# A graph network's second layer: attention scores scaled four tiles at a time and scattered from the features' block

## What is computed

```python
Qh = (x @ Wq + bq).reshape(N, 8, 32)
Kh = (x @ Wk + bk).reshape(N, 8, 32)
Vh = (x @ Wv + bv).reshape(N, 8, 32)
s = einsum('nhc,nhc->nh', Qh, Kh) / sqrt(32)      # one score for a node and head
alpha = leaky_relu(s[src] + s[dst], 0.2)          # edges, and one loop for each node
e = exp(alpha - segment_max(alpha, dst)[dst])
a = e / segment_sum(e, dst)[dst]
attn = segment_sum(Vh[src] * a[:, :, None], dst)
```

## Time and profile before

| | us |
|---|---|
| median of 3 runs | 2505.18 |
| lowest and highest | 2496.7, 2505.32 |
| the profiled execution's own time | 2504.01 |
| its span (first to last instruction) | 2502.2 |
| busy: PE, DVE, Pool, ACT | 1745.7, 1753.9, 1411.1, 597.9 |
| mean granted TensorE clock, as a share of full speed | 0.859 |

### The profile page before, as it was taken

One profiled execution on the slowest core, in us unless ns is written; L12 is line 12 of the kernel. 1 busy time (PEld: TensorE's weight loads), 2 busy tenths in 40 slices (PEclk: granted clock), 3 DMA queues, 4 the chain that ended last, 5 costly groups with the idle time before them and its releaser, 6 DMA issues. The chain is left out here.

```text
span 2502.2 us, 36831 instructions
## 1 busy us (share of the span) xinstructions
PE 1745.7 (70%) x10655; PEld 1385.5 (55%) x10655; DVE 1753.9 (70%) x2694; ACT 597.9 (24%) x1285; POOL 1411.1 (56%) x1456
## 2 busy tenths in 40 slices
PE   2698016788665654999987999020588899758498
PEld 1576014566444443899886777020456666547487
DVE  6688714899655557555686888970479999877675
ACT  2465100000000003455423333040011111124464
POOL 4377877777777772000006777887777777720050
PEclk9799556999978787899988999565789999979799
DMA  4166454666433342000022667536466666430100
GB/s 152 46 192 223 161 175 124 209 211 205 120 106 106 106 105 69 1 1 0 18 80 74 206 203 248 167 102 218 121 211 212 207 212 209 142 99 1 40 12 34
DMA packets 118702, 320.74 MB, mean 128 GB/s; under 512 B 37112, under 2 KB 63120, under 8 KB 104810
## 3 DMA queue, kind: packets, MB, share of 16 engines
q0 software_dynamic: 62272, 170.01, 23.8%
q1 hardware_dynamic: 55754, 145.31, 16.4%
q10 hardware_dynamic: 608, 4.59, 0.5%
HBM read 248.70 MB, written 71.12 MB: 128 GB/s over the span
## 5 line engine op out<-in xcount | busy, mean ns | idle before, releaser
L1214 PE MATMUL ms_ps_m<-ms_msg,ms_pick 128*128 128x260 f32 (+1 forms) x2816 | 794.5, 434 | 392.1 <-DVE ms_msg L1197 189.3
L804 POOL DMA_INDIRECT e_ring<-table,e_index x840 | 795.4, 947 | 257.8 <-issue 254.7
L1214 PEld LDWEIGHTS ms_ps_m<-ms_msg,ms_pick 128*128 128x128 f32 x2816 | 572.4, 212 | 613.9 <-issue 511.8
L1197 DVE TENSOR_TENSOR ms_msg<-e_ring,ms_ps_w 128x1040 f32 (+1 forms) x352 | 438.8, 1247 | 338.4 <-SPq L1138 338.4
L843 POOL DMA_INDIRECT e_ring<-table,e_stage_index x416 | 474.2, 1140 | 125.9 <-issue 120.6
L694 PE MATMUL sc_ps_e<-sc_keys,sc_hot 125*128 125x100 bf16 (+1 forms) x3840 | 290.2, 229 | 7.4 <-DVE all_xn L642 4.3
L694 PEld LDWEIGHTS sc_ps_e<-sc_keys,sc_hot 125*128 125x128 bf16 x3840 | 254.7, 98 | 54.0 <-DVE all_xn L642 25.1
L1180 DVE SCALAR_TENSOR_TENSOR ms_pick<-graph_dst_col,graph_tile_base,ms_ps_lane 128x512 f32<-128x512 f32 x352 | 263.2, 748 | 0.8 <-DVE all_acc L1167 0.8
L642 DVE TENSOR_REDUCE all_xn<-sc_ps_e 128x800 f32 (+1 forms) x240 | 236.0, 985 | 17.9 <-PE sc_ps_e L694 12.0
L605 ACT ACTIVATE sc_rows<-sc_ps_b 125x512 bf16<-125x512 f32 x320 | 173.0, 596 | 248.6 <-PE sc_ps_b L682 223.9
L1189 DVE TENSOR_TENSOR all_acc<-all_acc,ms_ps_m 128x260 f32 (+1 forms) x352 | 152.0, 432 | 55.2 <-PE ms_ps_m L1214 55.0
(11 more groups left out here) (423 smaller groups left out, 2652.1 us busy)
## 6 DMA issues: line engine op xcount, KB each, us to landing
ahead<-e_ring SPq DMA_DIRECT2D x32, 1056.0 KB, 4.6
e_ring<-ahead SPq DMA_DIRECT2D x32, 1056.0 KB, 5.1
ahead<-e_ring SPq DMA_DIRECT2D x20, 1040.0 KB
e_ring<-ahead SPq DMA_DIRECT2D x20, 1040.0 KB, 5.2
e_ring<-table,e_index POOLq DMA_INDIRECT x840, 2.8
e_ring<-table,e_stage_index POOLq DMA_INDIRECT x416
w_w<-L_ffn_w SPq DMA_DIRECT2D x2, 2048.0 KB
table<-qkv_v SPq DMA_DIRECT2D x5, 528.0 KB, 3.0
```

What stands on the lines that cost most here:

```text
L804: pool.indirect_dma_start(out=g.ring[:, slot * QUAD + i // GT, i % GT, :], out_offset=None, in_=s.table[:, :], in_offset=bass.IndirectOffs ...
L1197: dve.tensor_tensor(msg[:, b, :, 0:R].rearrange("p t (h o) -> p t h o", h=H), ring[:, bass.ds(slot, 1), :, :].rearrange("p a t (h o) -> p ...
L1214: mm = pe.matmul(ps_m[q % BANKS][:, 0:W], pick[:, b, t, :], msg[:, b, t, :], start=t == 0, stop=t == GT - 1)
```

## The change

The scatter of one tile's scores becomes a function, `place_score`. For layer one nothing moves: `edge_scores` calls it 20 times at the head of Pool's list as before. For layer two (`placed` is true there) `edge_scores` leaves it out, and Pool has a list of its own in the features' block: for each group of four tiles it waits for `score_ready` and issues four scatters. DVE scales four tiles at a time, after the fourth one's sum, in place of all 20 at the end, and each scaling counts `score_ready` up by one; the splitting and SP's store of the scores wait for all five. The numbers that are computed are the same.

```diff
--- before.py
+++ after.py
@@ -555,7 +555,13 @@
                 sp.wait_ge(h_out, 16 * (NT // step + 1))
 
 
-def edge_scores(nc, s, block, between, stage, tag, edge, parts, node, node_dram, line, dst_line, dst_start, H):
+def place_score(pool, line, first_edge, node, a, scattered):
+
+    pool.indirect_dma_start(out=line[:, :], out_offset=bass.IndirectOffsetOnAxis(ap=first_edge[:, a:a + 1], axis=0),
+                            in_=node[:, a, :], in_offset=None).then_inc(scattered, 16)
+
+
+def edge_scores(nc, s, block, between, stage, tag, edge, parts, node, node_dram, line, dst_line, dst_start, H, placed):
 
     C = HI * H
     SLOT = P if C <= P else 2 * P
@@ -581,9 +587,9 @@
 
         @block.gpsimd
         def _(pool):
-            for a in range(NT):
-                pool.indirect_dma_start(out=line[:, :], out_offset=bass.IndirectOffsetOnAxis(ap=s.first_edge[:, a:a + 1], axis=0),
-                                        in_=node[:, a, :], in_offset=None).then_inc(scattered, 16)
+            if not placed:
+                for a in range(NT):
+                    place_score(pool, line, s.first_edge, node, a, scattered)
             pool.indirect_dma_start(out=dst_start[:, :], out_offset=None, in_=node_dram[:, :],
                                     in_offset=bass.IndirectOffsetOnAxis(ap=s.chunk_dst[:, :], axis=0)).then_inc(scattered, 16)
 
@@ -1548,10 +1554,19 @@
                     dve.tensor_tensor(q_row[:, b, :], q_row[:, b, :], k_row[:, b, :], ALU.mult).then_inc(qk_ready, 1)
                     dve.wait_ge(qk_ready, a + 1)
                     dve.tensor_reduce(score[:, a, :], q_row[:, b, :].rearrange("p (h o) -> p h o", o=O), AX.X, ALU.add).then_inc(dot_ready, 1)
-                dve.wait_ge(dot_ready, NT)
-                link(dve.tensor_scalar(score[:, :, :], score[:, :, :], float(O) ** -0.5, None, ALU.mult))
-                dve.sem_inc(score_ready, 1)
+                    if a % SUB == SUB - 1:
+                        dve.wait_ge(dot_ready, a + 1)
+                        tiles = slice(a - SUB + 1, a + 1)
+                        dve.tensor_scalar(score[:, tiles, :], score[:, tiles, :], float(O) ** -0.5, None, ALU.mult).then_inc(score_ready, 1)
+                dve.wait_ge(score_ready, NB)
                 split_scores(dve, link, score, parts, rest)
+
+            @block.gpsimd
+            def _(pool):
+                for a in range(NT):
+                    if a % SUB == 0:
+                        pool.wait_ge(score_ready, a // SUB + 1)
+                    place_score(pool, s.lines[1], s.first_edge, score, a, s.scattered["sc1"])
 
             @block.sync
             def _(sp):
@@ -1562,7 +1577,7 @@
                 for a in range(0, NT, step):
                     sp.wait_ge(v_ready, a + step)
                     sp.dma_start(node_view(s.table[a * P:(a + step) * P, :]), v[:, a:a + step, :, :].rearrange("p a h o -> p a (h o)")).then_inc(v_out, 16)
-                sp.wait_ge(score_ready, 1)
+                sp.wait_ge(score_ready, NB)
                 sp.dma_start(node_view(s.dst_scores[1]), score[:, :, :]).then_inc(v_out, 16)
                 sp.wait_ge(v_out, 16 * (NT // step + 2))
 
@@ -2324,7 +2339,7 @@
 
         with nc.Block() as block:
             picks = edge_scores(nc, s, block, between, stage, "sc" + layer, edge, parts, node, s.dst_scores[int(layer)], s.lines[int(layer)],
-                                dst_line, dst_start, H)
+                                dst_line, dst_start, H, placed=self_loops)
             backs = edge_weights(nc, s, block, between, g, stage, picks, "wt" + layer, edge, dst_line, dst_start, acc, weight, H, self_loops)
             pass_messages(nc, s, block, between, g, stage, backs, "ms" + layer, weight, most, acc, H, loads)
```

## The result

| | before | after |
|---|---|---|
| median of four runs each, us | 2505.25 | 2482.53 |
| lowest and highest, us | 2496.7, 2507.59 | 2478.11, 2484.72 |
| profiled execution, us (span) | 2504.0 (2502.2) | 2478.11 (2476.3) |

The ratio is 0.9913 with a 95% interval of 0.9885 to 0.9942: the change makes the kernel 22.7 us faster. Forecast were 2481.0 us, with 2471 to 2490 as the range.

What follows compares the result with a forecast made beforehand. Pool's unbroken stream of some 886 us in layer two's edge work was taken as the bound. Head gain 26.2 us less 2.0 us late start gives 24.2 us: median 2505.2 becomes 2481.0 us, range 2471 to 2490.

Steps and rivals of the forecast that it cites:

- The bound: Layer two's edge block: Pool's unbroken stream of some 886 us bounds it, with the block's end behind it.
- The head: Start of Pool's edge-block stream: 3.56 us instead of 29.78, a gain of 26.2 us; gather 2.52 us beside DVE's clearing.
- DVE's scaling and the hidden 16: Features' block: five scalings priced at nothing, at most 1.2 us; the first 16 scatters hidden beside DVE's tiles.
- The delay of the block: Features' block end: the last four scatters start the edge block 2.0 us late, bounds 0.9 and 5.2.
- the rival that I gave 9%: Features' block exit waits until the last scatter's write has landed: delay 5.2 us, 2484.2 us in all; chance 9%.
- To the end: From stream to kernel end: the 24.2 us shift survives whole; 35 us of DVE's wait for rows remain.
- The clock: Rival, TensorE's granted clock: 0.03 either way is 8.3 us, giving 2473 or 2489; chance 15%, both sides alike.
- The number: Whole kernel: median 2505.2 becomes 2481.0 us, range 2471 to 2490; the forecast itself has 68%.
- The marks for the first Pool instruction and the dense part: Signs in the changed profile: edge block's first Pool instruction near 1324, with some 2.5 us; dense part near 2193.6.
- Pool does not take the port: Rival, features' block: Pool takes the port from DVE, lengthening the block by 13 us, 2494 us; chance 4%.
- their issue does not back up: Rival, features' block: scatters back up beside SP's stores; at 4 us each, 2520 us; chance 2%.
- The scores' chain: Rival, edge block: gathers delay index-pair loads by more than the 35 us left, shift worth nothing, 2505 us; chance 2%.

Runs made afterwards that it cites:

- The late scatters: Changed kernel with all 20 scatters in the features' block but behind the last tile's scaling: 2503.79 us, ratio 0.9987 to the kernel before.
- the run with eight pieces: Changed kernel with DVE clearing the buffer of pairs by eight instructions instead of one, in both layers: 3414.84 us, one execution.
- the scaling alone: Changed kernel with the 20 scatters back at the head of the edge block, scaling by fours kept: 2505.42 us, ratio 0.9994 to the kernel before.
- single tiles: Changed kernel with the last four tiles scaled and scattered one by one: 3416.22 and 3437.26 us, ratios 0.9953 and 0.9966 to the kernel before.
- the last two sets: Eight later runs in two sets: kernel before 3435.27 and 3444.47 us, changed kernel 3418.09 and 3429.94 us, ratios 0.996 and 0.9936.
- a clearing of its own: Changed kernel with Pool clearing an unused 128x640 tile behind its last scatter in the features' block: 3442.73 us, one execution.
- an explicit wait for the landing: Changed kernel with Pool waiting at the end of its features' list until all 20 scatters have landed: 2483.91 us, one execution.
- the kernel with sixteen scatters: Changed kernel with 16 scatters in the features' block, the last four at the edge block's head: 2485.16 us, ratio 0.9919 to the kernel before.
- the first set: Earlier runs, the first four experiments beside the kernel before, which took 2506.5 us there (median of 19).

## Why the prediction was right

**The bound.** Right. Pool's stream moved as a whole: first stage gather 25.23 us earlier, first message 25.3, last gather 25.4, dense part 25.5. The late scatters confirm it from the other side: with no overlap the gain is gone.

**The head.** Right to 0.01 us: 3.57 against 3.56, with 2.52 for the gather beside the clearing. The Trainium skill ("SBUF — State Buffer", who interferes with whom) had the clearing not contend, if it runs outside the two-port modes; the run with eight pieces shows that the single one does hold Pool's DMA, and the measurement decides.

**DVE's scaling and the hidden 16.** Right: five scalings of 0.18 us in the idle time of 0.29, ratio 0.9994 with the scaling alone, groups 8.64 us apart.

**The delay of the block.** This is the step that failed, in size and in cause. I took 2.0 us, with the casts holding Pool; it is 2.9. The casts do not hold it: the four scatters take 0.95, 0.95, 0.96 and 0.95 us. I had said that every row of such an overlap shows nearly full holding, but that held for the long instructions I had picked: in the kernel before, gathers of 0.95 us lie beside DVE's reductions of 0.98 us (L642). The unhindered Pool ends at 1320.24, 4.98 us behind the store, and it is the exit that comes late: 2.89 us behind Pool's last scatter, where I had carried over the 1.13 us that stood behind SP's landing.

What the exit follows is the landing of Pool's last write, and this is the rival that I gave 9%. In nine executions, with bursts of 4 and of 20 scatters and with a single one, Pool's DRAIN ends 0.86 to 0.87 us behind the last landing, while its distance from the last scatter's end goes from 1.99 to 3.88 us. This is read from the traces; no run moved the landing alone. It could have been seen before: where Pool leaves an early block behind its gathers of L386, in the kernel before, the DRAIN ends at 63.26, 0.86 us behind their last landing. The rival's price of 5.2 us was wrong: it set the 2.8 us from issue to landing behind the scatter's end, which it had put late for the casts. The last scatter landed 2.1 us behind its issue, 1.1 behind its end. The delay goes with the scatters near the block's end: none there, no delay; one, 1.0 us; a group of four, 2.9. My bounds of 0.9 to 5.2 held the value, and that 2.0 came out near it is luck, for its cause was another.

**To the end.** The change's own gain is 23.3 us against 24.2 in the forecast. DVE's wait for rows is 37.4 us against 35: its chain from the clearing to the clearing of the sums took 1678.56 - 1322.97 = 355.6 us against 358.1, 2.5 us less. With the scatters back at the head (the scaling alone) it took 355.9, so the scatters' place is not what shortened it; what did is open. Since DVE waits there in any case, it changes nothing. The clock is what it was in every stretch, so this rival did not come in.

**The number.** 2505.2 - 23.3 = 2481.9, and the median is 2482.53. Of the 25.9 us of the profiled executions, 1.8 are chance in their start. The four runs of each kernel spread over 7 and 11 us, so the times alone could not have told a delay of 2.0 from one of 2.9. The marks for the first Pool instruction and the dense part (1324 and 2193.6; seen 1323.14 and 2192.32) were missed by 0.9 and 1.3 us: the early start pulled them one way and the longer delay the other.

The other rivals fell too. DVE's tiles kept 2.16 us with scatters beside them, so Pool does not take the port. The scatters took 1.26 us each beside SP's stores, so their issue does not back up. The scores' chain did not become the bound: PE was busy for 195.94 us there as against 196.48, and DVE still waited 37.4 us for rows.

## What to carry over

Where one engine issues small DMAs back to back through a whole layer, look at its idle time in the stage before: work whose input grows there tile by tile fits into it, and each group costs only what stands behind the last tile. Count the exit of the block from what lands last, and by engine: the next block began 1.1 us behind SP's landing and 1.8 behind that of Pool's last write, though Pool's list has no wait for that landing. Look at the queue's own instructions (here the DRAIN) before you call an exit unexplained. An engine that issues DMAs can also be held by a neighbour's long instruction, and cutting that instruction up freed it here. And when you count a gain from one mark to another, look also at what the edit did ahead of the first mark: single tiles gave 1.9 us behind the store and cost over 3 ahead of it.

## What the runs showed of the hardware

**Leaving a block.** With DMAs of Pool near the block's end, Pool's DRAIN ends 0.86 to 0.87 us behind the landing of the last one (nine executions), and Pool's next DMA comes 0.90 to 0.91 us later where it stands first in the next block (a copy that stands first, 0.26). From the end of the last scatter's instruction to Pool's next one this is 2.89 to 2.90 us behind a burst, in five executions of three kernels, with 4 and with 20 scatters, and 4.79 us when a single scatter came last, which landed 4.0 us behind its issue beside SP's store. Behind a clearing of its own and behind an explicit wait for the landing the DRAIN ends 1.22 and 1.89 us behind the landing. In the kernel with sixteen scatters, where SP leaves last, it is 0.70. At the end of layer two's edge block in the kernel before, behind the long stream of gathers, it is 3.5 us, so 0.86 is no fixed price either. With no DMA in the block Pool's DRAIN takes 0.04 us. SP as the last: 1.1 us from its landing to the next block.

**DVE and Pool's DMA instructions.** One clearing of 1.76 us stretches the Pool DMA beside it from 0.98 to 2.52 us, and an addition of 9.38 us a gather to 9.51. Eight clearings in 2.19 us, casts of 0.24, subtractions of 0.33 and the tiles' additions of 0.42 us don't stretch it (0.95 to 1.00). Length alone does not decide: DVE's reductions of 0.98 us (L642, L648) leave the gathers beside them at 0.95, and two comparisons in a row, 0.87 us together, lie beside a gather of 1.34. In the changed kernel's time lines:

```profile
1332.65 0.87 DVE L643 TENSOR_SCALAR sc_hot<-sc_rows,all_node_of 125x1024 bf16<-125x1024 bf16 x2
1333.00 1.34 POOL L849 DMA_INDIRECT e_ring<-table,e_stage_index  x1 [0.30 <-issue]
```

**The same program in the last two sets.** They took 3435 and 3444 us for the kernel before. A row of the changed kernel's groups in the first of them (line, count, busy, mean ns, idle time before):

```profile
L810 POOL DMA_INDIRECT e_ring<-table,e_index x840 | 797.9, 950 | 1181.2 <-DVE ms_msg L1203 910.0
```

Pool's gathers last as long as in the first set (950 ns against 947), but Pool waits 910 us for DVE's products, where it hardly waited at all, with 358.4 us as the longest. So Pool's stream is not the bound in these sets, and the change is worth 0.4 to 0.6% instead of 0.9. Much of DVE's and ACT's waiting there ends with something that the trace puts down to none of the core's own instructions (it writes "remote"): DVE waits 361.9 us in this way before its additions of L1195 and 298.9 before its comparisons of L643. In the traces of the kernel before and of the changed one at 2505 and 2482 us no wait has this label. Why the program runs so differently is open.
